# Turned minima as a row of q, written by DMA, in the second context attention

## What is computed

```python
q = (latents @ w_q.T).reshape(B, L, 16, 8)     # latents: layernorm(x), 256 rows an item
k, v = jnp.split(x @ w_kv.T, 2, axis=-1)        # x here: the context, 64 rows an item
attn = softmax(einsum('blhd,bshd->bhls', q, k) * 8 ** -0.5)
out = einsum('bhls,bshd->blhd', attn, v).reshape(B, L, 128) @ w_out.T + b_out
```

## Time and profile before

| what | us |
|---|---|
| three runs | 1638.7, 1642.84, 1642.35 |
| their median | 1642.35 |
| the profiled execution | 1642.86 |
| its span, first to last instruction | 1641.1 |
| TensorE busy in it | 1477.3 |
| VectorE, ScalarE, GpSimd busy | 1103.3, 1014.1, 497.3 |
| mean granted TensorE clock | 0.958 |

### The profile page before, as it was taken

One profiled execution on the slowest core, in us unless ns is written; L12 is line 12 of the kernel. 1 busy time (PEld: TensorE's weight loads), 2 busy tenths in 40 slices (PEclk: granted clock), 3 DMA queues, 4 the chain that ended last, 5 costly groups with the idle time before them and its releaser, 6 DMA issues. The chain is left out here.

```text
span 1641.1 us, 39731 instructions
## 1 busy us (share of the span) xinstructions
PE 1477.3 (90%) x11703; PEld 1127.0 (69%) x11751; DVE 1103.3 (67%) x3548; ACT 1014.1 (62%) x2723; POOL 497.3 (30%) x828
## 2 busy tenths in 40 slices
PE   6999999999999878779999968999989968997798
PEld 4777777777777656458888845565556537775597
DVE  5777677776777558756666637778877745772565
ACT  5777677776777546266666636666666645662354
POOL 4333233332333235123333222333223105531133
PEclk9999999999999988779999979999999989996999
DMA  6000000000000040001111110000000000000000
GB/s 209 2 0 0 0 0 0 0 0 0 0 0 0 2 167 26 14 15 44 45 42 45 37 51 14 14 13 11 8 13 13 6 1 1 2 2 1 1 26 26
DMA packets 34079, 34.77 MB, mean 21 GB/s; under 512 B 5601, under 2 KB 29793, under 8 KB 33249
## 3 DMA queue, kind: packets, MB, share of 16 engines
q1 hardware_dynamic: 29664, 25.07, 4.7%
q0 software_dynamic: 4352, 8.92, 2.2%
HBM read 25.07 MB, written 8.91 MB: 21 GB/s over the span
## 5 line engine op out<-in xcount | busy, mean ns | idle before, releaser
L596 POOL TENSOR_SCALAR a_prob<-a_prob,a_inv 128x128 f32<-128x128 f32 (+1 forms) x256 | 126.6, 504 | 359.8 <-DVE a_inv L496 359.8
L430 ACT ACTIVATE a_prob<-a_psS,a_low 128x128 f32<-128x128 f32 (+1 forms) x512 | 210.0, 436 | 0.0
L486 DVE CUSTOM_DVE_ANT_0 a_psS<-a_psS,a_bias 128x128 f32<-128x128 f32 (+1 forms) x512 | 167.9, 390 | 45.7 <-PE a_psS L308 32.0
L1784 ACT ACTIVATE a_probT<-a_psZ 128x512 f32<-128x512 f32 x256 | 138.9, 594 | 75.4 <-PE a_psZ L1570 75.4
L421 ACT COPY a_probT<-a_psT 128x384 f32<-128x384 f32 x256 | 123.5, 482 | 95.3 <-PE a_psT L352 93.9
L1867 DVE TENSOR_REDUCE a_low<-a_psS 128x4 f32<-128x1024 f32 x128 | 156.7, 1224 | 26.4 <-PE a_psS L1570 25.3
L352 PE MATMUL a_psT<-ident,a_prob 128*128 128x128 f32 x768 | 138.8, 290 | 2.9 <-ACT a_probT L421 2.8
L1311 POOL DMA_INDIRECT d_rows<-rows_dram,source x72 | 68.2, 947 | 193.6 <-PE e_psX L1393 143.9
L308 PE MATMUL a_psS<-a_qk 64*128 64x128 f32 (+1 forms) x1024 | 120.4, 354 | 1.7 <-ACT a_qk L413 0.7
L352 PEld LDWEIGHTS a_psT<-ident,a_prob 128*128 128x128 f32 x768 | 80.2, 141 | 54.2 <-issue 46.4
L430 ACT ACTIVATION_READ_ACCUMULATOR a_prob<-a_psS,a_low 128x1 f32 x512 | 113.3, 221 | 0.0
(11 more groups left out here) (359 smaller groups left out, 4198.6 us busy)
## 6 DMA issues: line engine op xcount, KB each, us to landing
sorted_out<-e_y SPq DMA_DIRECT2D x72, 64.0 KB, 1.6
in_lo<-in_gate_up SPq DMA_DIRECT2D x4, 1024.0 KB, 6.9
x<-in_x SPq DMA_DIRECT2D x8, 256.0 KB, 6.9
down<-in_down SPq DMA_DIRECT2D x1, 2048.0 KB, 15.1
rows_dram<-rows SPq DMA_DIRECT2D x8, 256.0 KB, 2.2
out<-x SPq DMA_DIRECT2D x8, 256.0 KB, 2.3
d_rows<-rows_dram,source POOLq DMA_INDIRECT x72, 2.7
a_sel_in<-in_sel SPq DMA_DIRECT2D x1, 1024.0 KB, 4.8
```

The costliest lines, as they stand in the source:

```text
L430: nc.scalar.activation(prob[:, 2 * (p % 4) + k, lo:hi], psS[:, u, lo:hi], ACT.Exp, bias=low[:, u, i:i + 1], scale=-1.0, accum_out=total[:, ...
L486: nc.vector.tensor_tensor_reduce(psS[:, u, lo:hi], psS[:, u, lo:hi], bias0[:, 2 * p + k, lo:hi], 1.0, LEAST, ALU.add, ALU.min, low[:, u, i ...
L596: nc.gpsimd.tensor_scalar(w, w, inv[:, 2 * (q % 2) + 1, i:i + 1], 1.0, ALU.mult, ALU.mult).then_inc(norm_done[1], 1)
L1784: nc.scalar.activation(probT[:, (p + half + 1) % 2, 2 * half + c, :, :].rearrange("p j s -> p (j s)"), psZ[:, c, :], ACT.Exp, scale=-1.0). ...
```

## The change

The minima are no longer added by a product. A row of each head that q leaves free, row 24 of its 32 (`MAX_ROW`), holds them instead: after `keep_lows`, SP issues four DMAs an item, one per group of four heads, each copying 4 partitions x 256 numbers (4 KB) from `low_cols` into rows 24, 56, 88 and 120 of q4. The key side gets -1 in these rows: `ck.minus` is -1 there and is the bias of the four copies that make `ck.k4`. So one product gives the score less the minimum. `turned_scores` waits on `max_in` (four semaphores, one for each of the four q4 buffers) in place of `cols_kept`. The product with `ck.pick`, the matrix itself (one ScalarE instruction) and the zeroing of `low_cols` (one VectorE memset) are gone; `low_cols` shrinks to 16 partitions. VectorE makes `ck.minus` with two small instructions. The natural scores see zero in row 24 of q, as the q copy leaves it, because the DMA comes after them. The q4 buffer is written by SP's DMAs before the turned scores read it.

The order on TensorE and ScalarE inside a slot is rewritten too:

```diff
@@ tensor: turned_scores @@
                 if half == 0:
-                    pe.wait_ge(cols_kept, m + 1)
+                    pe.wait_ge(max_in[at], 16 * G4 * (m // 4 + 1))
...
-                        pe.matmul(cols, k_bd[:, at, pair // 2, 2 * k:2 * k + 2, :], q4[:, at, pair // 2, :], start=True, stop=False)
-                        mm = pe.matmul(cols, ck.pick[:, 2 * pair:2 * pair + 2, :], low_cols[:, at % 2, :], start=False, stop=True)
+                        mm = pe.matmul(cols, k_bd[:, at, pair // 2, 2 * k:2 * k + 2, :], q4[:, at, pair // 2, :], start=True, stop=True)
@@ tensor: slot @@
                 if has(3):
                     turn_lows(n, n - 3, (p - 3) % 4)
+                if has(4):
+                    values(n - 4, p, 0)
+                    values(n - 4, p, 1)
                 if has(2):
                     natural(n - 2, (p - 2) % 4, 0)
+                if has(1):
+                    spread(n - 1, (p - 1) % 4, 0)
                 if has(4):
                     turn_values(n - 4)
-                if has(3):
-                    turned_scores(n - 3, (p - 3) % 4, 0)
-                if has(1):
-                    spread(n - 1, (p - 1) % 4, 0)
                 if has(2):
                     natural(n - 2, (p - 2) % 4, 1)
-                if has(4):
-                    turn_rows(n - 4)
                 if has(0):
                     if has(3):
                         pe.wait_ge(cols_kept, n - 2)
                     project(n)
-                if has(3):
-                    turned_scores(n - 3, (p - 3) % 4, 1)
                 if has(1):
                     spread(n - 1, (p - 1) % 4, 1)
                 if has(3):
-                    values(n - 3, (p - 3) % 4, 0)
+                    turned_scores(n - 3, (p - 3) % 4, 0)
+                if has(4):
+                    turn_rows(n - 4)
+                if has(3):
+                    turned_scores(n - 3, (p - 3) % 4, 1)
                 if has(4):
                     output(n - 4)
-                if has(3):
-                    values(n - 3, (p - 3) % 4, 1)
@@ scalar: slot @@
+                if has(3):
+                    keep_lows(n - 3, (p - 3) % 4)
                 if has(4):
                     keep_values(n - 4)
-                if has(3):
-                    keep_lows(n - 3, (p - 3) % 4)
-                    exps(n - 3, 0)
                 if has(1):
                     keep_q4(n - 1, (p - 1) % 4, 0)
                 if has(0):
                     keep_hi(n, p)
+                if has(3):
+                    exps(n - 3, 0)
+                if has(1):
+                    keep_q4(n - 1, (p - 1) % 4, 1)
                 if has(4):
...
                 if has(3):
                     exps(n - 3, 1)
-                if has(1):
-                    keep_q4(n - 1, (p - 1) % 4, 1)
@@ sync @@
+        @block.sync
+        def _(sp):
+            for m in range(B):
+                sp.wait_ge(cols_kept, m + 1)
+                for G in range(G4):
+                    sp.dma_start(q4[MAX_ROW:P:P // 4, m % 4, G, :].bitcast(F32), low_cols[4 * G:4 * G + 4, m % 2, :].bitcast(F32)).then_inc(max_in[m % 4], 16)
@@ layer1_attention: scalar, vector @@
-                nc.scalar.activation(ck.pick[:], g.ident[:, 0:H].unsqueeze(2).to_broadcast([P, H, L]), ACT.Copy, scale=-1.0).then_inc(pick_set, 1)
...
+                act.wait_ge(minus_set, 2)
...
-                    nc.scalar.copy(ck.k4[:, G, :], (psZ if G % 2 else psS)[:].rearrange("p c s -> p (c s)")).then_inc(ck4_kept, 1)
+                    nc.scalar.activation(ck.k4[:, G, :], (psZ if G % 2 else psS)[:].rearrange("p c s -> p (c s)"), ACT.Identity,
+                                         bias=ck.minus[:], scale=1.0).then_inc(ck4_kept, 1)
...
+                v.tensor_reduce(ck.at_max_row[:], g.ident[:].rearrange("p (h r) -> p h r", h=4)[:, :, MAX_ROW], AX.X, ALU.add).then_inc(minus_set, 1)
+                dve.wait_ge(minus_set, 1)
+                v.tensor_scalar(ck.minus[:], ck.at_max_row[:], -1.0, None, ALU.mult).then_inc(minus_set, 1)
```

More of the change, by code:

```diff
@@ L38 @@
 START = 1
+MAX_ROW = 24
 SLOPES0 = (1.0 / np.power(np.float32((2.0 ** 8) ** (1.0 / H)), np.arange(1, H + 1, dtype=np.float32))).astype(np.float32)
@@ L1512, in layer1_attention @@
             "oc_kept", "y_done", "y_used", "xb_done", "act_seen", "dve_seen", "pool_seen", "ck_done", "ck_hi_done", "ck_lo_done",
-            "cv_done", "cv_kept", "ck4_done", "ck4_kept", "own_set", "pick_set")}
+            "cv_done", "cv_kept", "ck4_done", "ck4_kept", "own_set", "minus_set")}
         (sel_loaded, sel_ready, line_loaded, v_zero, v_one, low_zero, bq_ready, cur_ready, proj_done,
@@ L1517, in layer1_attention @@
          oc_kept, y_done, y_used, xb_done, act_seen, dve_seen, pool_seen, ck_done, ck_hi_done, ck_lo_done,
-         cv_done, cv_kept, ck4_done, ck4_kept, own_set, pick_set) = sem.values()
+         cv_done, cv_kept, ck4_done, ck4_kept, own_set, minus_set) = sem.values()
         fetched = [ph.sem(f"fetched{i}") for i in range(4)]
@@ L2005, in __init__ @@
         self.v_rows = sb("v_rows", [P, B, D])
-        self.pick = sb("pick", [P, H, L], F32R)
+        self.at_max_row = sb("at_max_row", [P, 1])
+        self.minus = sb("minus", [P, 1])
         self.own = sb("own", [P, 4])
@@ L2038, in layer1_context @@
         low = ph.sb("low", [P, 2, BT, H])
-        low_cols = ph.sb("low_cols", [P, 2, S], F32R)
+        low_cols = ph.sb("low_cols", [H, 2, S], F32R)
         probT = ph.sb("probT", [P, PAIRS, S])
@@ L2044, in layer1_context @@
         o_cols = ph.sb("o_cols", [P, S])
-        (q_done, hi_done, lo_done, spread_done, q4_kept, kbd_ready, s_done, low_done, lowt_done, cols_zero, cols_kept, z_done,
+        (q_done, hi_done, lo_done, spread_done, q4_kept, kbd_ready, s_done, low_done, lowt_done, cols_kept, z_done,
          exp_done, v_zero, v_one, v_ready, pv_done, o_kept, ot_done, inv_done, o_norm, oc_done, oc_kept, y_done, y_used,
          x_biased, seen, pool_seen, act_seen) = (ph.sem(name) for name in (
-            "q_done hi_done lo_done spread_done q4_kept kbd_ready s_done low_done lowt_done cols_zero cols_kept z_done "
+            "q_done hi_done lo_done spread_done q4_kept kbd_ready s_done low_done lowt_done cols_kept z_done "
             "exp_done v_zero v_one v_ready pv_done o_kept ot_done inv_done o_norm oc_done oc_kept y_done y_used "
             "x_biased seen pool_seen act_seen").split())
+        max_in = [ph.sem(f"max_in{i}") for i in range(4)]
         ln = LayerNorm(ph, g, "ln")
@@ L2213, in keep_lows @@
                 act.wait_ge(lowt_done, m + 1)
-                if isinstance(m, int) and m < 2:
-                    act.wait_ge(cols_zero, 1)
-                else:
+                if m >= 2:
                     act.wait_ge(z_done, m * 4 - 4)
-                nc.scalar.copy(low_cols[0:H, at % 2, :], psT[0:H, 0:S]).then_inc(cols_kept, 1)
+                nc.scalar.copy(low_cols[:, at % 2, :], psT[0:H, 0:S]).then_inc(cols_kept, 1)
             def exps(m, half):
@@ L2262, in _ @@
             v.memset(v_bd[:], 0.0).then_inc(v_zero, 1)
-            v.memset(low_cols[:].bitcast(F32), 0.0).then_inc(cols_zero, 1)
             dve.wait_ge(v_zero, 1)
```

## The result

The changed kernel takes 1667.19 us (median of 4 runs, 1665.8 to 1668.54), the kernel before 1642.59 beside it. The ratio is 1.0155, with a 95% interval of 1.0137 to 1.0173: 1.55% slower. The profiled execution took 1665.8 us.

The account below looks back on a forecast made before the run. TensorE was the fullest engine in the second context attention, but the new order's ring would set the slot: 12 x 0.80 = 9.6, plus 1.5 and 1.9 at the ends, 13.0 us; forecast 1655.5 us, range 1641 to 1667.

Parts of the forecast that it names:

- The new order's ring: Chain of steps and waits between LayerNorm turns in second context attention: 8.77 us a slot against 7.97; chance 0.60, flight covered.
- the turned minima into the value products: Start of the slot on TensorE, LayerNorm turn and turned minima before the value products: 0.41 us.
- the second natural scores: Four TensorE products after VectorE's minimum frees the PSUM tile: 4 x 0.12 = 0.48 us.
- for x: End of slot: with value products moved, TensorE waits bare for VectorE's addition to x, some 0.8 us.
- the output columns: ScalarE's copy of the output columns, 0.37 us in the sum; TensorE was to wait about 0.5 us for it.
- The product's price: Removing eight pick-matrix products a slot from TensorE: 0.94 us a slot, 15 us over 16 slots.
- exposed flight: Rival: DMA landing over 2.4 us brings rows later than 4.7 us after the minima; 1660 to 1669 us, chance 0.17.
- a rival with 0.02: Rival: with more waits TensorE could be granted half its clock; above 1675 us, chance 0.02.
- the three short distances: Between turned minima, the first two and the last distances: +0.5 us each, 1.5 us.
- the drain: After the last minima nothing covers the DMA flight, so the last turned scores start later: +1.9 us.
- the case that I thought likeliest: Longer ring with the DMA flight covered: 1650 to 1661 us, chance 0.60.
- The edits at nothing: Pick matrix removal, bias on four k4 copies, two tiny VectorE operations, dropped memset: bounded by 0.3 us either way.

Follow-up runs that it names:

- e1: Kernel before, pick products kept and no DMA, with the changed kernel's order on TensorE and ScalarE; slot 9.12 us, ratio 1.0094.
- e4: Changed kernel without its DMAs, minimum not subtracted in the turned scores, which wait for the copy of the minima; slot 8.89 us, ratio 1.0144.
- e11: Changed kernel with ScalarE copying the output columns before the second q copy; slot 8.40 us, ratio 1.0066.
- e6: Changed kernel with turned output rows before turned scores, output columns copied before exponentials, output product between the halves of turned scores; slot 7.43 us, ratio 0.9974.
- e9: The order of e6 on the changed kernel, with the projection also ahead of the second natural scores; slot 7.03 us, ratio 0.9925.
- e3: Kernel before without the pick products and without DMAs, minimum not subtracted in the turned scores, old order; slot 7.05 us, ratio 0.9929.
- e5: Changed kernel with six extra unused products a slot in TensorE's wait for the addition to x; slot 8.89 us, ratio 1.0094.
- e13: Changed kernel with two extra unused products a slot in TensorE's wait for the addition to x; slot 8.89 us, ratio 1.0100.
- e7: Kernel before, pick products kept and no DMA, with its own new order on TensorE and ScalarE; slot 7.17 us, ratio 0.9940.
- e10: Kernel before, pick products kept and no DMA, in exactly the order of e9; slot 7.30 us, ratio 0.9979.

## Why the prediction was right or wrong

- **The direction and its cause were right.** The new order's ring sets the slot; e1 (no DMA, no clock fall, 9.12 us) and e4 (no DMA, 8.89 us) show it with the other causes taken away, and e11, e6 and e9 by shortening it. The forecast slot was 8.77 us, measured 8.89. The terms that were short are the turned minima into the value products (0.59 against 0.41, though the value products behind them took 1.00 for 1.14, so most of that is a shift between two terms) and the second natural scores (0.57 against 0.48, the first after a wait). Within the sum TensorE's waits were shorter than I had them: 0.66 us for x (0.8), 0.40 for the minimum (0.5), 0.26 for the output columns (0.5), but 0.29 more for the first exponentials.
- **The product's price was right.** 0.94 us forecast, 0.92 in e3. (8 x 0.12 is 0.96, and the chances for slower add to 0.79, not 0.78; neither moves the forecast.)
- **The DMA was right in the slot.** I had the rows in q 3.9 us after the minima; it was 4.2 (0.93 to the first issue, not 0.85; issues 0.54 us apart, not 0.47; landing 1.67, not 1.6), under a cover of 4.7 (measured 1442.78 to 1447.63: 4.85). The chance of 0.17 for an exposed flight was not needed.
- **The step that failed is that the clock was put at nothing in the sum, as a rival with 0.02.** I let one stretch of before stand for the new slot: 18.96 of 27 us busy and still 1.00. The windows of before for the end of that stretch and for what follows it show what the earlier trace rows leaves out, and an earlier stretch shows the same:

```profile
1542.00:1546.00 4.00, 1.20 (x9) 1.04 (x9) 1.60 (x4) 0.50 (x2) 0.00 (x0) 0.98 0.00 0
1546.00:1549.40 3.40, 3.40 (x8) 2.71 (x9) 0.50 (x2) 0.90 (x2) 0.00 (x0) 0.52 0.02 5
...
587.00:610.00 23.00, 20.13 (x109) 15.46 (x107) 16.51 (x52) 13.03 (x30) 6.72 (x14) 1.00 0.42 172
610.50:620.70 10.20, 9.05 (x33) 7.14 (x33) 8.14 (x23) 5.82 (x13) 6.32 (x9) 0.51 0.09 26
```

The clock fell to 0.52 at its very end, at 1546.0, where TensorE was busy again, behind a stretch of 4 us with 1.2 us of work. A stretch at 1.00 that ends in a fall is evidence against, not for. From 587 to 610 us TensorE was busy for a larger part (20.13 of 23 us) than in the new slots at the full clock (33.86 of 41.90), and the clock fell at 610.5 all the same; there the last 2.5 us were idle. The busy share of a long stretch could not tell. In the changed kernel the falls came in the loaded part, four times, and cost 5.3 us; e5 shows 5.2 us coming back when they are gone. (The two figures agree less well than they look: the last slot hit takes 8.44 us in e5, not 8.89, which makes the cost 5.8, and the fill of e5 adds 0.7 to the second distance.) The "above 1675" that I gave this rival came from no sum.
- **The ends were sized too low.** I gave 1.5 us to the three short distances and 1.9 to the drain, 3.4 in all. The first two distances grew by 0.5 and 1.1 and the last by 1.3, 2.9; the drain by 3.9. Together 6.8. Of the drain I had only the later start of the scores. The half clock also covers 14.9 us of this drain, 8.1 of the drain before; what that costs is not taken apart.
- The sum: 12 distances by 0.92 for 0.80, +1.4; clock +5.3; ends +3.4; earlier stages -1.0. 13.0 + 9.1 = 22.1, against 22.7 measured (the third distance, 7.64 before, grew by 0.3 more than the 0.92). The time of 1667.19 lies just above the range, which ended at 1667, and 6 us above the 1650 to 1661 of the case that I thought likeliest; without the falls it would be about 1662. That the range came so near is owed to its upper end, which I had put there for the exposed flight, and this did not come.
- The edits at nothing are not seen: the stage starts 1.0 us earlier in this profile, and the runs on one chip differ by up to 4 us ahead of it. No run takes them apart.

## What to carry to other kernels

In a hand-ordered pipeline like this one, price a new order before the operation that it serves: follow the ring of waits once round, from starts in the timeline, and ask for each wait what stood in it before. A step that ends in a buffer's release (here the output columns, the output product, the addition to x) went first on both engines in the faster orders here (e11, e6), and the exponentials behind it. And when a change takes work from the fullest engine and leaves it short waits, look at the granted clock: a few products that compute nothing paid for themselves here (e5, e13), though a shorter ring gained more (e11, e6, e9).

## What the runs showed of the hardware

- The granted clock fell to 1.2 GHz for 3.4 us at a time in slots whose like at the full clock has no idle time on TensorE over 0.66 us, in four slots of the changed kernel (twice measured), eight of e4, none of e1, e3, e5, e6, e7, e9, e10 and e11. The same 0.66 us of idle time is in the slots of e1 and e11. Which slots are hit varies; a slot of 8.89 us that is hit is 1.3 to 1.7 us longer.
- Two more 128x256 products a slot, 0.24 us of 8.89, went with no fall in the steady part (e13, one profile).
- A copy of 4 x 1 KB from SBUF to SBUF occupied SP for 0.50 us, issues came 0.54 us apart, and the last was usable 1.67 us after its issue.
